# Attention on one Trainium2 core: value products of two steps in one row, four step buffers, the bias rows issued by ScalarE, more blocks pooled

## What is computed

```
layer 0: y = softmax(q k^T / sqrt(32), causal) v + softmax(qc kc^T / sqrt(32)) vc   # 1024 keys; 2048 context keys
layer 1: y = softmax(q k^T / sqrt(32)) v                                           # 2048 context keys
x = x + tanh(gate) * (y W + b)                                                     # 2 batches, 16 heads of 32 columns
```

## Time and profile before

| | |
|---|---|
| median of 3 runs | 4381.48 us (4379.73 to 4384.93) |
| the profiled execution | 4377.09 us, span 4375.5 us |
| PE busy in the span | 3873.5 us (89%) |
| DVE, ACT, POOL busy | 2522.5 us (58%), 2009.5 us (46%), 1417.7 us (32%) |
| attn0, first to last score | 472 to 1707 us |
| attn1, first to last score | 2463 to 3376 us |

### The profile page before, as it was taken

The page is one execution under the profiler, slowest core; times in us unless marked ns, Lnnn a source line. Parts: engine busy times, 40 slices in busy tenths (PEclk is TensorE's granted clock), DMA queues, the critical chain, the costliest instruction groups (busy, mean ns, idle before and its releaser), DMA issues. The chain is left out here.

```text
span 4375.5 us, 79396 instructions
## 1 busy us (share of the span) xinstructions
PE 3873.5 (89%) x32204; PEld 2714.2 (62%) x32204; DVE 2522.5 (58%) x2758; ACT 2009.5 (46%) x3511; POOL 1417.7 (32%) x718
## 2 busy tenths in 40 slices
PE   7989699999999997739996599999998739999997
PEld 5777456665665664429895355555555427888886
DVE  4345567767776773466664577777764464343342
ACT  2222256666666664016662266666655004444332
POOL 0000265555555554001110356666555000111110
PEclk9999699999999998759998799999999759999999
DMA  5478524423441431426663633322210413443331
GB/s 169 161 257 285 132 51 110 111 67 73 106 102 50 103 68 66 144 89 208 206 204 102 163 74 74 74 61 65 63 38 18 145 48 128 130 118 117 110 109 38
DMA packets 278320, 485.28 MB, mean 111 GB/s; under 512 B 21904, under 2 KB 117136, under 8 KB 269840
## 3 DMA queue, kind: packets, MB, share of 16 engines
q1 hardware_dynamic: 263952, 443.40, 35.3%
q0 software_dynamic: 14080, 37.76, 3.7%
HBM read 350.67 MB, written 130.02 MB: 110 GB/s over the span
## 5 line engine op out<-in xcount | busy, mean ns | idle before, releaser
L810 DVE TENSOR_REDUCE attn_parts<-attn_mx 128x4 f32<-128x2048 f32 (+2 forms) x608 | 1342.1, 2207 | 629.0 <-PE attn_mx L674 523.7
L780 ACT ACTIVATE attn_probs<-attn_sc 128x512 f32<-128x512 f32 (+1 forms) x2368 | 1227.7, 595 | 615.4 <-PE attn_sc L704 546.3
L658 POOL TENSOR_TENSOR attn_psums<-attn_psums,attn_probs 128x1024 f32<-128x1024 f32 x408 | 970.6, 2379 | 149.9 <-ACT attn_probs L780 115.6
L704 PE MATMUL attn_sc<-attn_queries,attn_keys 97*128 97x256 f32 (+1 forms) x4736 | 922.8, 313 | 50.2 <-DMA attn_queries<-attn_topT 42.8
L704 PEld LDWEIGHTS attn_sc<-attn_queries,attn_keys 97*128 97x128 f32 x4736 | 668.7, 193 | 402.9 <-issue 224.0
L721 PE MATMUL attn_acc<-attn_probs,attn_values 128*32 128x256 f32 x9472 | 644.9, 391 | 1.9 <-ACT attn_probs L780 1.4
L655 POOL TENSOR_TENSOR attn_psums<-attn_probs 128x1024 f32<-128x1024 f32 x80 | 190.6, 2382 | 790.2 <-ACT attn_probs L780 790.2
L1425 DVE TENSOR_TENSOR ffn_wL<-ffn_raw,ffn_wH 128x2048 fp32r<-128x2048 f32 x128 | 293.4, 2292 | 224.0 <-ACT ffn_wH L1380 222.7
L674 PE MATMUL attn_mx<-attn_keysn,attn_queriesn 32*128 32x512 f32 (+2 forms) x2432 | 312.5, 503 | 101.4 <-DVE attn_parts L810 72.8
L1380 ACT ACTIVATE ffn_wH<-ffn_raw 128x2048 fp32r<-128x2048 f32 x128 | 245.3, 1916 | 338.8 <-DMA ffn_raw<-in_L_ffn_W_dram 177.9
L721 PEld LDWEIGHTS attn_acc<-attn_probs,attn_values 128*32 128x32 f32 x9472 | 250.6, 110 | 188.9 <-issue 12.2
(11 more groups left out here) (190 smaller groups left out, 4424.9 us busy)
## 6 DMA issues: line engine op xcount, KB each, us to landing
ffn_raw<-in_L_ffn_W_dram SPq DMA_DIRECT2D x128, 1024.0 KB, 5.4
attn_keys<-l_cross_keys SPq DMA_DIRECT2D x48, 1024.0 KB, 12.7
attn_queries<-l_queries SPq DMA_DIRECT2D x48, 512.0 KB, 17.9
l_cross_keys<-projc_high SPq DMA_DIRECT2D x64, 256.0 KB
l_cross_keys<-projc_lowp SPq DMA_DIRECT2D x64, 256.0 KB
l_cross_values<-projc_vout SPq DMA_DIRECT2D x64, 256.0 KB
attn_keysn<-l_cross_keys SPq DMA_DIRECT2D x16, 1024.0 KB, 5.0
attn_values<-l_cross_values SPq DMA_DIRECT2D x64, 256.0 KB, 23.3
```

The lines of the kernel that those rows point to most:

```text
L658: pool.tensor_tensor(ps, ps, at, ALU.add).then_inc(added, 1)
L704: mm = pe.matmul(out[:, n0:], KS[b][0:3 * HD + 1, h, kb * P:(kb + 1) * P], QS[b][0:3 * HD + 1, h, job.qb * QB + n0:(job.qb + 1) * QB], sta ...
L780: act.activation(probs[:, m % RING, i // 2, heads, n0:], sc[:, item % SC, :].rearrange("p (h q) -> p h q", q=QB)[:, :, n0:], ACT.Exp, scal ...
L810: dve.tensor_reduce(parts[j % ROWS_DEEP][:, :, t, part], mx[:, :, 0:cols], AX.X, ALU.max).then_inc(max_read, 1)
```

## The change

Four things change in the attention stages.

1. `Plan.values_at` collects the steps in pairs (a job's last step closes a pair), and a row m runs the value and ones products of both steps of the pair that ended with m-1, or none. Rows by turns are "empty" and "full": an empty row is score 0, the groups, scores 1, 2, the turns, score 3; a full one scores 0, 1, the groups, score 2, the products of two steps, the turns, score 3. Which groups and turns stand in which row is as before.
2. `RING` goes from 3 to 4 step buffers of probabilities, `DEEP` (output buffers) from 6 to 5.
3. Ten instead of eight blocks of a cross job are pooled (0 to 4, 6, 7, 8, 10, 12 instead of 0, 1, 2, 4, 6, 8, 10, 12), and in causal jobs all unmasked ones (0, 2, 4, 6 instead of 0, 0, 3, 4).
4. `set_row` moves from SyncE to ScalarE, behind exponent 3 of the row with the turn. The pieces of `load_stack` go out two or three per row.

```diff
--- before.py
+++ after.py
@@ -412,8 +412,7 @@
                 cols = min(BLK, n - part * BLK)
                 self.groups.append((t, part, cols, unit.causal and part == self.parts - 1))
         whole = [kb for kb, n0, masked in self.blocks if not masked]
-        inner = [kb for kb in whole if kb < len(self.blocks) - 3]
-        self.pooled = [kb for kb in inner if kb < 2 or kb % 2 == 0] if len(inner) > 2 else []
+        self.pooled = whole if unit.causal else [kb for kb in whole[:-3] if kb < 4 or kb == 7 or kb % 2 == 0]
 
     def adds(self, step=None):
 
@@ -460,6 +459,11 @@
                 self.place(done, m)
                 done += 1
         assert done == len(due)
+        self.values_at, held = {m: [] for m in range(n + 1)}, []
+        for m in range(n):
+            held.append(m)
+            if len(held) == 2 or self.ends(m) is not None:
+                self.values_at[m + 1], held = held, []
         self.item, self.turn_item, k = {}, [0] * len(self.jobs), 0
         for j in self.turn_at[-1]:
             self.turn_item[j], k = k, k + 1
@@ -518,7 +522,7 @@
     plan = Plan(units)
     jobs, N_STEPS, N_JOBS = plan.jobs, plan.steps, len(plan.jobs)
     KEYS = max(u.keys for u in units)
-    RING, SC, DEEP = 3, 3, 6
+    RING, SC, DEEP = 4, 3, 5
     ROWS = GH * QB // P
     with Phase(nc, name) as ph:
         KS = [ph.sb(f"keys{b}", [P, GH, KEYS], F32R) for b in range(BUFS)]
@@ -577,17 +581,6 @@
         with nc.Block() as block:
             @block.sync
             def _(sp):
-                def set_row(j):
-                    job = jobs[j]
-                    sp.wait_ge(exped, plan.turn_item[j] + 1)
-                    if job.u >= BUFS:
-                        sp.wait_ge(valued, plan.last_of[job.u - BUFS] + 1)
-                    q0 = job.qb * QB
-                    for t in range(QB // P):
-                        sp.dma_start(QS[job.u % BUFS][3 * HD:3 * HD + 1, :, q0 + t * P:q0 + (t + 1) * P].bitcast(F32),
-                                     topT[t * GH:(t + 1) * GH, j % TOPS, :].bitcast(F32)
-                                     ).then_inc(row_set[j % ROWS_DEEP], DMA)
-
                 def store(j):
                     d, job = j % DEEP, jobs[j]
                     sp.wait_ge(normed, j + 1)
@@ -600,21 +593,18 @@
                     load_stack(sp, 0, piece)
                 for piece in range(FLAT):
                     load_flat(sp, 1, piece)
-                for j in plan.turn_at[-1]:
-                    set_row(j)
                 for piece in range(STACK):
                     load_stack(sp, 1, piece)
                 for m in range(N_STEPS + 8):
                     if 0 <= m - 7 < N_STEPS and plan.ends(m - 7) is not None:
                         store(plan.ends(m - 7))
-                    for j in plan.turn_at.get(m, ()):
-                        set_row(j)
                     for u in range(len(units) - BUFS):
                         piece = m - max(plan.unit_max_at[u], 0) - 1
                         if 0 <= piece < FLAT:
                             sp.wait_ge(max_ready, plan.unit_groups[u])
                             load_flat(sp, u + BUFS, piece)
-                        for piece in range(2 * (m - plan.last_of[u] - 1), 2 * (m - plan.last_of[u])):
+                        pace = STACK // min(STACK, units[u + 1].keys // BLK + 1)
+                        for piece in range(pace * (m - plan.last_of[u] - 1), pace * (m - plan.last_of[u])):
                             if 0 <= piece < STACK:
                                 sp.wait_ge(valued, plan.last_of[u] + 1)
                                 load_stack(sp, u + BUFS, piece)
@@ -747,12 +737,15 @@
                 for m in range(N_STEPS + 1):
                     if m < N_STEPS:
                         scores(m, 0)
-                        scores(m, 1)
+                        if plan.values_at[m]:
+                            scores(m, 1)
                         for k in plan.groups_at[m]:
                             maxima(k)
+                        if not plan.values_at[m]:
+                            scores(m, 1)
                         scores(m, 2)
-                    if m:
-                        values(m - 1)
+                    for step in plan.values_at[m]:
+                        values(step)
                     if m < N_STEPS:
                         for j in plan.turn_at[m]:
                             turn(j)
@@ -767,6 +760,17 @@
                         act.wait_ge(row_set[(j - TOPS) % ROWS_DEEP], ROW * DMA * ((j - TOPS) // ROWS_DEEP + 1))
                     act.activation(topT[:, j % TOPS, :], sc[0:ROWS, item % SC, 0:P], ACT.Copy, scale=-1.0
                                    ).then_inc(exped, 1)
+
+                def set_row(j):
+                    job = jobs[j]
+                    act.wait_ge(exped, plan.turn_item[j] + 1)
+                    if job.u >= BUFS:
+                        act.wait_ge(valued, plan.last_of[job.u - BUFS] + 1)
+                    q0 = job.qb * QB
+                    for t in range(QB // P):
+                        act.dma_start(QS[job.u % BUFS][3 * HD:3 * HD + 1, :, q0 + t * P:q0 + (t + 1) * P].bitcast(F32),
+                                      topT[t * GH:(t + 1) * GH, j % TOPS, :].bitcast(F32)
+                                      ).then_inc(row_set[j % ROWS_DEEP], DMA)
 
                 def exponent(m, i):
                     job, item = jobs[plan.job_of[m]], plan.item[m, i]
@@ -790,6 +794,8 @@
 
                 for j in plan.turn_at[-1]:
                     turned(j)
+                for j in plan.turn_at[-1]:
+                    set_row(j)
                 for m in range(N_STEPS + 1):
                     if m < N_STEPS:
                         for i in range(3):
@@ -800,6 +806,8 @@
                         for j in plan.turn_at[m]:
                             turned(j)
                         exponent(m, 3)
+                        for j in plan.turn_at[m]:
+                            set_row(j)
 
             @block.vector
             def _(dve):
```

## The result

| | before | changed |
|---|---|---|
| median | 4382.8 us (4 runs) | 4578.3 us (4 runs, 4571.3 to 4580.8) |
| ratio | | 1.0449 (95%: 1.0437 to 1.0462) |
| span of the profiled execution | 4375.5 us | 4576.2 us |

What follows compares the result with a forecast made beforehand. It took the single tile `mx`, spacing groups of maxima at least 2.91 us apart, as the bound over PE. attn1 +51, attn0 +79 and clock 10 gave +140 on 4377.1, said as 4520 us; range 4440 to 4600.

Steps and rivals of the forecast that it cites:

- The chain of maxima: Attention: single tile `mx` keeps groups of maxima at least 2.91 us apart; cross job 26.2 to 28.4 us, +136 us.
- the short gap: From an empty row's group of maxima to the full row's: 1.81 us of PE work, held to 2.91 us.
- the long one: From a full row's group of maxima to the next: 3.43 us of PE work plus 0.43 per block of ones.
- Causal units: Four merged pairs each, about +0.6 per pair, less 1.7 for fewer ones products: +0.7 x 8 units = 5 us.
- Rows on ScalarE, what it removes: attn1: PE's late waits for rows behind SyncE's loads end, about 9 us each, six times: -54 us, bounds 0 and -57.
- the six late rows: attn1 turns where PE waits for row DMAs behind the value loads, mean wait 6.3 us, predicted to go.
- the rival of 0.10: Loads fill the DMA engines or ScalarE is held at issue, so rows stay late: -54 not won, about 4575; chance 0.10.
- Rows on ScalarE, what it adds: Issues delay exponentials and row data land late: +1.2 x 31 = 37 us in attn1, 6 us in attn0.
- the sign "one of about 2 at each first item of a job": Expected in attn1's new timeline: a PE wait for rows of about 2 us there, instead of 6 us.
- Clock: Attention: new PE waits of 1.1 us cause ten stretches at 1.2 GHz, 10 us; bounds 0 and 60.
- one wait of 2.40 us: PE wait between two groups of maxima that left PEclk at 1.00 from 741.2; used to argue for few clock falls.
- The range: Whole kernel: 4440 to 4600 us, from free ScalarE issues with clock at 0 to late rows with part of the clock.

Runs made afterwards that it cites:

- x2: Kernel before with the pairing of steps alone and the four step buffers it needs: 4612.4 us, ratio 1.0537.
- x3: Changed kernel with VectorE reducing only the first half of each group of maxima: 4470.8 us.
- x4: Changed kernel with a full row's group of maxima behind score 2 instead of before it, no work added or removed: 4508.3 us.
- y2: Changed kernel with each score matmul of cross jobs between an empty row's group and the full row's issued twice: 4568.5 us.
- z3: Kernel before with the changed pooling alone, in cross and causal jobs, three step buffers, rows by SyncE: 4393.5 us, ratio 1.0032.
- x1: Changed kernel with one step's values in every row again, all else as changed: 4382.4 us, ratio 1.0006 to the kernel before.
- z4: Kernel before with stack loads in two parts, ten pooled blocks in cross jobs only, four step buffers: 4305.6 us, ratio 0.9836.
- z1: Kernel before with stack loads split in two parts by a wait where the next unit is a cross one: 4325.3 us, ratio 0.9882.
- z2: Changed kernel with stack loads split in two parts by a wait where the next unit is a cross one: 4549.9 us.

## Why the prediction was right, and where its terms were off

- *The chain of maxima.* Right, and the main term. The prediction gave 2.91 us for the short gap and 3.43 plus ones for the long one; the changed kernel has 2.90 and 3.40, 3.83, 4.28, 5.13 with zero, one, two and four products of ones (the last four are three blocks and the pooled sum). A cross job was to grow from 26.2 to 28.4; its gaps are 26.4 and 28.2, without what the turn costs on ScalarE. One count was wrong: the change saves 640 products of ones, not 672, since the causal jobs with two pooled blocks now need a pooled sum; the terms of the sum use the right count. x2, x3 and x4 show it from three sides: added alone, the chain shortened, the work moved across it.
- *Causal units.* +5 forecast, -2 in the gaps. Their ends wait for GpSimd: 8.0 us in eight waits in attn0 (bounds 0 and 16, 0 taken).
- *Rows on ScalarE, what it removes.* This step failed. -54 was forecast from the end of the six late rows; the waits themselves fell from 37.9 us to 26.7, and with what follows a late row some 16 us of the 54 came. The prediction took the lateness for SyncE's queue. It was two things, the queue and the DMA engines being full, and the second alone keeps the row late. This was the rival of 0.10, and the trace of before held it: while SyncE's issues and a store stood for 22 us the DMA engines were full too (share 1.04 from 2588 to 2613). The page DMA: Bandwidth & Descriptors of the Trainium skill, under Issuing engines are not separate DMA queues, says that the DMAs of all issuers run on the same 16 engines; by that rule the trace agrees, with the share at 1.04 until the row landed. That rival's time, about 4575, is met by luck: it charged all of the 54 to the rows, where they cost 38, and the clock made up the rest.
- *Rows on ScalarE, what it adds.* 37 us in attn1 were forecast, the gap behind a turn 4.1 us. It is 3.33: 0.42 x 31 = 13 us. The first exponential runs beside the issues, and a row away from loads needs 0.75 us behind its issue by its packets, less than the 2.0 us that I had read beside them. So the sign "one of about 2 at each first item of a job" did not come either. Not forecast at all: 9 us at the start of attn0, where the first rows now stand among the loads of unit 1, and 4 at the start of attn1.
- *Clock.* 10 us, with bounds 0 and 60, for a term that is near 70. This is the largest miss in size. The prediction argued from one wait of 2.40 us that left the clock up. That row was the exception. The kernel before has eight such waits in the cross units of attn0, and behind seven of them the clock is at 1.2 GHz within 2 us; one of the seven, and the window behind it:

```profile
894.83 0.50 PE L674 MATMUL attn_mx<-attn_keysn,attn_queriesn 32*128 32x512 f32 x4 [2.40 <-DVE attn_parts L810]
896.20:899.60 3.40, 3.40 (x30) 1.95 (x22) 1.48 (x1) 1.02 (x3) 0.00 (x0) 0.50 0.00 0
```

  The fall at 763.1, which I had put down to nothing, also has a wait of PE for VectorE just ahead of it (0.78 us, to 762.40). So the trace of before already tied the falls to waits in the chain of maxima, and y2 shows it for the new ones: with the short gap filled the falls go from 58 to 17.
- *The range.* 4578 lies 22 us under its end. The profiled executions are 201 us apart where 140 were forecast. Against the forecast stand the clock (+60), the failed gain of the rows (some +38), the starts of the stages (+13), the ScalarE term (-24), the maxima (-20) and the causal units (-7): together 60. That terms counted too high made up for almost half of those counted too low is luck. The excess can't be told apart more closely than that.

What stays open: how a wait leads to a stretch at 1.2 GHz of one length or another, and why some lead to none. z3's and x1's falls in attn0 go with the causal pooling (z4 has none of it and keeps 0.96). GpSimd's waits at the ends of causal jobs stand ahead of the longest stretches behind unit 0, but not of all falls, and no run took these waits away alone.

## What to carry to other kernels

Where a tile exists once, what counts is the work between its two uses: share it out evenly before merging anything, since the short side waits and the long side pays. A busy share near 100% doesn't show such a floor; a row with less work that is not shorter by as much does. What a wait does to the clock is not read from one row: look at all its like in the trace. An order by row numbers doesn't pace a queue that has nothing to wait for; loads that must leave a time free for a small urgent transfer need a wait that says so.

## What the runs showed of the hardware that was not expected

- Work added to an idle gap cost nothing: some 2500 matmul instructions more, 58 falls of the clock to 1.2 GHz down to 17, 10 us less, which is at the edge of the noise (y2).
- A DMA of 2 KB on a queue of its own landed 6.1 us after its issue beside loads of 256 KB to 1 MB on another queue; its last packet ended 4.0 to 5.4 us after the issue there and 0.75 us after it away from them. With the loads timed away from it the wait was gone (z1, z2).
- A DMA issue on ScalarE holds its queue for 0.6 us, as on SyncE, but an exponential that was already started (2825.54, 0.60 us) runs on beside it (2825.61).
- In the kernel before, seven of eight waits of 2.40 us by PE were followed within 2 us by a stretch at 1.2 GHz.
